# |w| tiles of a two-stage kernel spread anew over its stages, with three staging slots, and the last query blocks ordered by token block

## What is computed

```python
q = x @ Wq.T + bq;  k = x @ Wk.T + bk;  v = x @ Wv.T + bv      # 16 query heads, 4 kv heads, D = 128
sq, sk = elu(q) + 1, elu(k) + 1
kv = einsum('bhsd,bhse->bhde', sk, v);  k_sum = sk.sum(tokens)
attn = einsum('bhsd,bhde->bhse', sq, kv) / (sq . k_sum + 1e-6)
x = layernorm(x + attn @ Wo.T)

def absmean_quant(w):                    # ternary: -1, 0, 1
    scale = mean(abs(w))
    return sign(w) * (abs(w) >= 0.7 * scale)
h = gelu(x @ absmean_quant(w1).T + b1)                          # 2048 -> 8192
x = layernorm(x + h @ absmean_quant(w2).T + b2)                 # 8192 -> 2048
```

## Time and profile before

| | us |
|---|---|
| three runs | 2660.42, 2953.24, 2958.25 (median 2953.24) |
| profiled execution | 2657.98 |
| its span, slowest core (6) | 2656.4 |
| spans of the 8 cores | 2642.0 to 2656.4 |
| busy in the span: PE / DVE / ACT / POOL | 2506.3 / 892.9 / 608.0 / 274.2 |
| matmuls in the profile | 11628 |
| moved by DMA | 481.73 MB, mean 181 GB/s |

### The profile page before, as it was taken

The page is one execution under the profiler, slowest core; times in us unless marked ns, Lnnn a source line. Parts: engine busy times, 40 slices in busy tenths (PEclk is TensorE's granted clock), DMA queues, the critical chain, the costliest instruction groups (busy, mean ns, idle before and its releaser), DMA issues.

```text
span 2656.4 us, 30067 instructions; the slowest of 8 cores (2642.0 to 2656.4 us)
## 1 busy us (share of the span) xinstructions
PE 2506.3 (94%) x11628; PEld 1141.5 (43%) x11780; DVE 892.9 (34%) x906; ACT 608.0 (23%) x823; POOL 274.2 (10%) x333
## 2 busy tenths in 40 slices
PE   5999999978987988979999999999999999999998
PEld 1444444434443433334444444444444444444443
DVE  1222444425553444455577557311000000110022
ACT  0233677723333333321100000011121110000000
POOL 3000000013332000000122112100000000000000
PEclk9999999989999999989999999999999999999999
DMA  9984786677778887865688768527113110312252
GB/s 164 227 220 147 184 204 186 175 206 269 259 257 285 298 294 292 298 230 182 220 281 274 225 217 267 176 87 245 36 40 102 38 32 8 111 64 80 78 184 111
DMA packets 93339, 481.73 MB, mean 181 GB/s; under 512 B 11920, under 2 KB 11920, under 8 KB 50576
## 3 DMA queue, kind: packets, MB, share of 16 engines
q1 hardware_dynamic: 49824, 310.97, 35.3%
q0 software_dynamic: 33008, 145.77, 19.7%
q10 hardware_dynamic: 10368, 23.07, 3.3%
HBM read 431.53 MB, written 85.98 MB: 195 GB/s over the span
## 4 chain that ended last, share of the span: by engine, by line
PE 72%; DMA 19%; issue 4%; DVE 3%; ACT 1%; POOL 0%; ACTq 0%; SPq 0%; DVEq 0%; POOLq 0%
PE PB L617 27%; PE PB L595 22%; DMA MB<-w2h 14%; PE PB L515 8%; PE PB L631 4%; PE PB L488 4%; PE PB L478 4%; PE PB L552 2%; DMA R<-woh 2%; DMA MA<-w1h 1%; DMA RW<-wvh 1%; ACT MB L849 1%; DVE R L713 1%; DVE MB L710 1%; PE PB L503 0%
## 5 line engine op out<-in xcount | busy, mean ns | idle before, releaser
L617 PE MATMUL PB<-R 128*128 128x512 fp8e4 x2688 | 582.7, 379 | 0.3 <-DVE R L713 0.3
L595 PE MATMUL PB<-R,MC 128*128 128x512 bf16 x2006 | 450.3, 383 | 32.2 <-DVE MC L713 27.2
L617 PEld LDWEIGHTS PB<-R 128*128 128x128 bf16 x2688 | 262.8, 98 | 318.0 <-issue 1.2
L595 PEld LDWEIGHTS PB<-R,MC 128*128 128x128 fp8e4 x2048 | 200.0, 99 | 281.5 <-issue 50.4
L794 DVE TENSOR_TENSOR MC<-PB,MC 128x512 f32<-128x512 f32 x56 | 38.3, 684 | 822.2 <-PE PB L617 728.1
L595 PE MATMUL PB<-MA,MC 128*128 128x512 bf16 x1004 | 229.9, 379 | 1.1
L595 PE MATMUL PB<-MB,MC 128*128 128x512 bf16 x1003 | 229.9, 379 | 1.1
L515 PE MATMUL PB<-R,MB 128*128 128x512 bf16 x1003 | 229.5, 379 | 1.1
L710 DVE TENSOR_SCALAR MB<-MA,thr 128x2048 fp8e4<-128x2048 f32 x107 | 137.6, 1286 | 252.1 <-DMA MA<-w1h 146.3
L943 ACT ACTIVATE R<-PB,b_sb 128x512 bf16<-128x512 f32 x192 | 128.3, 684 | 402.5 <-PE PB L595 402.5
L849 ACT ACTIVATE MB<-MB 128x2048 f32<-128x2048 f32 x70 | 133.7, 1910 | 378.6 <-DMA MB<-w2h 336.9
(11 more groups left out here) (108 smaller groups left out, 1747.4 us busy)
## 6 DMA issues: line engine op xcount, KB each, us to landing
MA<-w1h SPq DMA_DIRECT2D x122, 1024.0 KB, 7.5
MB<-w2h SPq DMA_DIRECT2D x85, 1024.0 KB, 6.7
MA<-w2h SPq DMA_DIRECT2D x43, 1024.0 KB, 7.9
R<-xb POOLq DMA_DIRECT2D x32, 512.0 KB, 75.8
x1s<-R POOLq DMA_DIRECT2D x16, 1024.0 KB, 7.1
w1qd<-MC POOLq DMA_DIRECT2D x64, 256.0 KB, 5.2
MC<-w1qd SPq DMA_DIRECT2D x64, 256.0 KB, 2.6
R<-w2qd SPq DMA_DIRECT2D x16, 1024.0 KB, 5.8
```

What stands on the lines that cost most here:

```text
L595: ins = e.matmul(PB[F1_BANK[k % 4][t]], w1q_sb(k)[:, dc * 128:(dc + 1) * 128], x1T(s, t, dc), start=(dc == 0), stop=(dc == 15))
L617: ins = e.matmul(PB[F2_BANK[P][cc]], hid(fc)[:, c * 128:(c + 1) * 128], w2q_sb(s, g, q)[:, j * 512:(j + 1) * 512], start=(fc == 0), stop=( ...
```

## The change

1. |w| is dealt out anew: 32 tiles behind the k/v blocks (one each from block 6 on, two from block 26 on), 40 behind the projections (every second, and one more behind n = 6, 14, 22, ...), 24 behind Wo's items (every second up to 38, then 44, 50, 56, 62), and the last 32 tiles as 64 half tiles of 128 x 1024 in FFN1, three in two steps, until step 42. `wsum` has a column for each.
2. Slots: tiles 0 to 71 as before in MA's two; tiles 72 to 91 go through three, MA's two and MB's; 92 to 95 through MB's. The half tiles have three slots in MB, of which the third is the buffer of the cast `x1bf` and is loaded only after the last transposes.
3. The last three heads of the q stage (ic 13, 14, 15) are projected by token block: all three for t = 0, then t = 1, and so on. Their order is `QORD`.
4. Wo's second half goes to the blocks 0 and 1 of x and is asked for after projections 55 and 58; the residual slots move to blocks 2 and 3.
5. Wo's items begin with two chunks by column halves instead of three; threshold 1 is made at item 10; the first four w1 tiles are made ternary behind items 48, 52, 56 and 60.

```diff
-NW_KV = 26
-NW_Q = 32
-NW_WO = 32
-NW_F = 128 - NW_KV - NW_Q - NW_WO
+NW_KV = 32
+NW_Q = 40
+NW_WO = 24
...
+def w_behind_q(n):
+    a = NW_KV + n // 2 + (n + 1) // 8
+    return range(a, NW_KV + (n + 1) // 2 + (n + 2) // 8)
...
+def w_behind_f(k):
+
+    return range(min(NW_HALF, 3 * k // 2), min(NW_HALF, 3 * (k + 1) // 2))
...
+QORD = [(ic, t) for ic in range(13) for t in range(4)]
+QORD += [(ic, t) for t in range(4) for ic in range(13, 16)]
...
+ITEMS = [(0, 0), (0, 1), (1, 0), (1, 1), (0, 2), (0, 3), (1, 2), (1, 3)]
+ITEMS += [(c, g) for c in range(2, NCH) for g in range(4)]
...
-THR1_ITEM = 22
+THR1_ITEM = 10
 W1_PRE = 4
-PRE_ITEM = [36, 40, 44, 48]
+PRE_ITEM = [48, 52, 56, 60]
...
+    def stage_half(u):
+        o = (0, 1024, 3072)[u % 3]
+        return mbf[:, o:o + 1024]
...
+        def load_w(i):
+            if W_PREV[i] >= 0:
+                e.wait_ge(a_abs, W_PREV[i] + 1)
+            e.dma_start(out=stage(w_slot(i)), in_=w_tile(i)).then_inc(d_st[w_slot(i)], 16)
+
...
+        def load_half(u):
+            if u < 2:
+                e.wait_ge(a_abs, NW_FULL)
+            elif u == 2:
+                e.wait_ge(t_tr, 2 * NCH)
+            else:
+                e.wait_ge(a_abs, NW_FULL + u - 2)
+            e.dma_start(out=stage_half(u), in_=w_half(u)).then_inc(d_h[u % 3], 16)
+
         for k in range(W1_PRE, NFC):
             e.wait_ge(v_w1, k - 1)
             e.dma_start(out=stage(k % 2), in_=w1h[k]).then_inc(d_st[k % 2], 16)
-            i = NW_ATT + NW_WO + k - W1_PRE
-            if i < 128:
-                e.wait_ge(a_abs, i)
-                e.dma_start(out=stage(2), in_=w_tile(i)).then_inc(d_st[2], 16)
+            if k == W1_PRE:
+                load_half(0)
+                load_half(1)
+            if k == W1_PRE + 1:
+                load_half(2)
+            if k >= 6:
+                for u in w_behind_f(k - 6):
+                    if u + 3 < NW_HALF:
+                        load_half(u + 3)
...
-                e.wait_ge(t_q, 62 + pr // 4)
+                e.wait_ge(t_q, 55 + 3 * (pr // 4))
```

More of the change, by code:

```diff
@@ L171, in wo_sb @@
     def wo_sb(ic, g):
-        base, o = (rw, 0) if g < 2 else (r1, 8192)
+        base, o = (rw, 0) if g < 2 else (r1, 0)
         o += ic * 1024 + (g % 2) * 512
@@ L176, in wo_pair @@
     def wo_pair(half, pr):
-        base, o = (rw, 0) if half == 0 else (r1, 8192)
+        base, o = (rw, 0) if half == 0 else (r1, 0)
         return base[:, o + pr * 2048: o + (pr + 1) * 2048]
     def yslot(c):
-        o = (0, 2048, 12288)[c % 3]
+        o = 8192 + (c % 3) * 2048
         return r1f[:, o:o + 2048]
@@ L255, in build_nc, with w_half @@
     p_id, p_b2 = sem("p_id"), sem("p_b2")
-    def n_slot(i, j):
-        return i // 2 + 1 if i < NW_ATT else i - NW_ATT + 1
-    def abs_slot(i):
-        return i % 2 if i < NW_ATT else 2
-    N_ST = [NW_ATT // 2, NW_ATT // 2, 128 - NW_ATT]
+    N_THR = [0, 5, 11]
+    N_W = [16 * (1 + sum(w_slot(b) == w_slot(i) for b in range(i))) for i in range(NW_FULL)]
+    W_PREV = [max([b for b in range(i) if w_slot(b) == w_slot(i)], default=-1) for i in range(NW_FULL)]
+    N_ST = [sum(w_slot(b) == j for b in range(NW_FULL)) for j in range(3)]
     def w_tile(i):
         return w1h[i] if i < 64 else w2h[(i - 64) // 16, (i - 64) % 16]
+    def w_half(u):
+        return w_tile(NW_FULL + u // 2)[:, (u % 2) * 1024:(u % 2 + 1) * 1024]
     def w1_load_no(k):
@@ L507, in tensor_program @@
         e.wait_ge(v_kb, NSC)
-        for n in range(64):
-            ic, t = n // 4, n % 4
+        for n, (ic, t) in enumerate(QORD):
             if n >= 3:
@@ L672, in normalise @@
             e.wait_ge(a_r, m + 1)
-            e.tensor_tensor(attn(m % 4, m // 4), PB[3 + m % 2], rn(m), ALU.mult).then_inc(v_at)
+            e.tensor_tensor(attn(QORD[m][1], QORD[m][0]), PB[3 + m % 2], rn(m), ALU.mult).then_inc(v_at)
         e.wait_ge(v_sv, NSC)
-        for n in range(64):
-            ic = n // 4
+        for n, (ic, t) in enumerate(QORD):
             e.wait_ge(a_eq, n + 1)
@@ L856, in scalar_program @@
             e.activation(ek(sc), kb1(sc), AF.Exp, bias=c_none).then_inc(a_e)
[L857 to L858 removed]
+            for i in w_behind_kv(sc):
+                abs_tile(i)
         def inverse(m):
@@ L879, in scalar_program @@
                 inverse(n - 3)
-            if n % 2 == 1:
-                abs_tile(NW_KV + n // 2)
+            for i in w_behind_q(n):
+                abs_tile(i)
         inverse(61)
@@ L909, in scalar_program @@
                 evict_x1T(ENDS[i - 4])
-            if i % 2 == 0:
-                abs_tile(NW_ATT + i // 2)
+            for w in w_behind_wo(i):
+                abs_tile(w)
         chunk_rstd(15)
@@ L946, in scalar_program @@
                     evict_x1T(15)
-                if s == 0 and k < NW_F:
-                    abs_tile(NW_ATT + NW_WO + k)
+                if s == 0:
+                    for u in w_behind_f(k):
+                        abs_half(u)
                 if s == 1 and k == 3:
```

96 lines of the change are left out of this document (59 added, 37 removed).

## The result

The changed kernel takes **2576.5 us** where the kernel before, beside it on the same chip, takes 2660 to 2665. The ratio is 0.966, 95% interval 0.963 to 0.969: 3.4% faster. The forecast was 2566 us, its range 2548 to 2600.

What follows compares the result with a forecast made beforehand. TensorE's matmuls bound the kernel, with some 64 us lost in FFN1 and 55 in Wo to waits and slower clock. 2658.0 - 52.4 (FFN1) - 49 (Wo) + 7.4 (q) + 2 (k/v) = 2566 us, range 2548 to 2600.

Steps and rivals of the forecast that it cites:

- threshold 2: FFN1's first half, step 48: TensorE waits 4.7 us for the ternary and then the sum, plus 2 us of slow clock.
- group 55: q stage: while Wo's second half streams, a landing takes 10 us, the tile is 4.4 late, 3.5 us at TensorE.
- x1T's wait: FFN1, before step 3: half 2 is asked for only after the last transposes, so TensorE waits 3.5 us.
- 38 x 1.2 = 46 of the 64: FFN1 before the change: 38 steps of 8.1 us instead of 6.9 make 46 of some 64 us lost.
- GpSimd's loop: Wo: add, store, wait and reload of residual slots takes 16.2 us against chunks of 14.7; 5 us allowed.
- The wait of group 63: End of the q stage: a late tile while Wo's second half streams makes TensorE wait 3 us.
- A: FFN1 becomes bound by w1's two slots, from a landing of 9.7 us; at 11, 28 us more: 2594; chance 0.13.
- B: Wo: POOL's residual loop bounds all 13 reloads at 16.2 us a chunk, 19.5 instead of 5: 2581; chance 0.10.
- C: q stage: 40 tiles through two slots make the kernel slower than before; at a landing of 18 us, 2713; chance 0.02.
- D: FFN1: halves each take a whole tile's 5.9 us, one behind another, 86 us more: 2652; chance 0.03.
- E: q stage: Wo's second half or the late triples of tiles cost double, about 15 us more: 2581; chance 0.06.
- F: Wo and q stage come without the prediction's allowances: 2550 us; chance 0.04.

Runs made afterwards that it cites:

- The experiment with one slot: Changed kernel with FFN1's last 32 tiles whole through one slot, each load asked for when the sum before is out: 2606.6 us, ratio 0.9772 to the kernel before.
- the run with q's tail moved: Changed kernel with the three tiles behind groups 54, 62 and 63 of the q stage moved into Wo (37 and 27 tiles): ratio 0.9647 to the kernel before.
- k/v spread: Changed kernel with the six extra k/v tiles behind blocks 20, 22, ... 30 instead of 26 to 31: ratio 0.9675 to the kernel before.
- with 31 tiles: Changed kernel with 31 tiles in the q stage instead of 40 and 33 in Wo instead of 24: ratio 0.9693 to the kernel before.
- 31 tiles and threshold 2 first: Changed kernel with 31 q tiles, threshold 2 ahead of the ternary, x1T copied out behind step 1: 0.967; with k/v's extra tiles spread too: 0.9664.
- four edits: Changed kernel with threshold 2 ahead of the ternary, k/v tiles spread, three q tiles in Wo, last x1T copied out behind step 1: 2562.4 us, ratio 0.961.

## Why the forecast was nearly right, and what it missed

**The step that failed: the slow clock behind the short waits.** The prediction priced it at one place only, 2 us behind threshold 2, and at nothing behind every other wait that it foresaw, in k/v, in q, in Wo and before step 3. On core 1 it was 2.7 us behind the last k/v products, 1.4 at group 55, 5.4 in Wo and 3.8 in FFN1, 13.3 instead of 2. These 11 us are as much as the 10.6 of gain that did not come; the other errors nearly cancel. The waits and the mechanisms were mostly those named. The first of the four is hidden in the q stage. TensorE's timeline on core 1, where the products had waited 3.36 us, and on core 0, where they had waited 0.95 (one matmul's record is missing there):

```profile
275.16 13.21 PE L577 MATMUL PB<-R,MB 128*128 128x512 bf16 x48
```

```profile
270.14 10.52 PE L577 MATMUL PB<-R,MB 128*128 128x512 bf16 x47
```

The first attention pair comes 13.05 us after the stage's start on core 1 and 10.36 on core 0. The granted clock of core 1 was 0.82 from 275.16 to 290.60 us, and 1.00 on core 0.

**FFN1, -52.4 forecast, -50.7 measured.** The sum of what stays was right in each term that has a row: a step of 6.95 us, x1T's wait 3.58 against 3.5 (2.9 to 4.7 by core), threshold 2's 4.68 against 4.7 on all eight cores. The clock was put at 2 and is 3.8 (455.1 - 443.0 - 3.58 - 4.68): it was counted behind the threshold and not behind x1T's wait. What the prediction said of the loss before, "38 x 1.2 = 46 of the 64", is wrong in size. The rows said so already: TensorE's waits for ternaries were 27.2 in 24, not 46. The experiment with one slot gives 24 for 32 steps, since the lead of the ternary tiles pays for the first steps. The forecast escaped this because it was built from what remains and not from what goes.

**The halves.** The price per half was the open question, and the rule on transfers under 1 MiB that the prediction cites spoke against them. The run with one load in flight shows that a half lands in 4.9 us where a whole tile takes 5.9, so a large part of a landing does not depend on size. A line through these two landings, with other traffic beside them, puts that part at 4.9 - (5.9 - 4.9) = 3.9 us, an estimate. The Trainium skill, DMA: Bandwidth & Descriptors, section Anatomy of one DMA, has such a fixed part, about 2 us, for transfers issued by GpSimd; these are issued by SyncE, and come out larger. The decision, that depth hides it, was right. The transfers were asked for two steps ahead, landed in 10.4 us each, and TensorE did not wait. That whole tiles with as many bytes in flight would have done as well is not excluded by any run.

**Wo, -49 forecast, -39.2 measured on core 1.** This is the term that was furthest off. Weights hidden: right, they were there at 543, before the item at 551.6. Chunks of 14.7 to 15.5: right for eleven of fourteen, all at 14.7; the other three are 16.2 to 18.2 apart. GpSimd's loop was no bound; the allowance of 5 us for it was met by one late residual, for which VectorE waited 10.8 us:

```profile
599.36 1.86 PE L593 MATMUL PB<-ident,MB 128*128 128x128 bf16 x16 [3.36 <-DVE MB L829]
601.01 8.97 PE L614 MATMUL PB<-RW,R 128*128 128x512 bf16 x32
```

Two things were not in the sum. The wait of group 63 (3.0 in the prediction's q stage, 4.18 here) falls behind the first Wo items, so it is Wo's, and the clock behind the small waits was priced at nothing. The second line above shows it: 32 matmuls in 8.97 us instead of 7.07. The same core after the other two (timelines, first column the start, second the length):

```profile
513.19 5.06 PE L577 MATMUL PB<-R,MB 128*128 128x512 bf16 x16
```

```profile
541.86 0.58 PE L564 MATMUL PB<-MC,ksrep 128*128 128x512 bf16 x1 [4.18 <-DVE R L735]
...
542.66 9.13 PE L614 MATMUL PB<-RW,R 128*128 128x512 bf16 x32
```

16 in 5.06 instead of 3.62, and 32 in 9.13: 1.4 to 2.1 us behind these waits of 2.6 to 4.2, where some matmuls ran at the 1.2 GHz level. Not every such wait has that cost: in the run with the old q order the wait of 2.65 before the first Wo item is followed by 16 matmuls in 3.61, at full clock. In the run with one slot, waits of 0.5 to 1.5 us were each followed by 32 matmuls in 7.07, with no such cost. Wo's 250.7 is 235.8 of work (core 0 of the run with q's tail moved: 238.0 less 2.2 of waits, at a granted clock of 1.00), 9.5 of waits and 5.4 of clock. The forecast had 235, 6 of waits and no clock. On the other cores Wo took 244 to 250; core 1 had the longest.

**q, +7.4 forecast, +4.4 measured.** The sum is nearly right by luck. Core 1 did not wait at groups 8, 16, 24 or 32 at all (forecast 3.6), and waited 2.58 at group 55 (forecast 3.5) with 1.4 of clock; group 63's wait is Wo's, and the 2.7 of clock behind k/v, which was not forecast, took its place. The 2.65 before the first Wo item went as forecast. Together that is 2.58 + 1.4 + 2.7 - 2.65 = 4.0 of the 4.4. At group 55 ScalarE had waited for its tile, whose load took 13 us beside the stream of Wo's weights (ScalarE's timeline):

```profile
507.70 1.91 ACT L918 ACTIVATE MA<-MA 128x2048 f32<-128x2048 f32 x1 [3.40 <-DMA MA<-w2h]
```

The prediction had 10 for it. Cores 2, 3 and 5 did wait near group 12, up to 3.2, but there by the debt from k/v. The experiments with k/v spread and with 31 tiles point to one cause behind both: 40 tiles in two slots are just too many for the core of two neighbours that has the longer landings, so a wait taken away in one place turns up in the next. Of two neighbours one has tile landings 0.2 to 1 us longer in q by their medians; that was the late one in all four pairs of the changed kernel, and in three of four when it ran again. The prediction read one core's landings as those of all.

**k/v, +2 forecast, +4.4 measured on core 1.** The last products wait 3.36 us there, 1 to 4 by core, where all cores had waited 0.95 before. So the wait grew by 2.4, near the forecast, and it goes when the tiles are spread: the mechanism (9 us for two tiles against blocks of 7.1) was right. Of the other 2.0 some 0.7 are waits for the first loads, and 1.3 are not accounted for.

**The missing 10.6 us** are then: 2.4 in k/v, 9.8 in Wo and 1.7 in FFN1, less 3.0 in q and 0.3 in the rest. Counted by cause, slow clock is 11 of them. With q's tail moved, the waits at the end of q and in Wo and the clock behind them go, and some 7.5 us with them. What is not settled is which neighbour is the late one and why it alternates from run to run.

**Rivals.** A: not in the changed kernel (w1's median 8.5); seen on one core of the fastest one and on five of each kernel with 31 tiles and threshold 2 first. B: no, but true with 33 tiles in Wo. C: no; the q stage stayed at 258 or less. D: no, and true with one load in flight. E: in small part; the two waits of q's end cost 10.3 us with their clock on core 1 where 6.5 were priced, not 15 more. F: 2550 without allowances is nearly what four edits reach, 0.961 of 2658, or 2554.

## What to carry to other kernels

Build a forecast from the work and waits that will remain, not from the loss you think goes: a chain that turns too slowly costs TensorE only from where its lead is used up. Splitting a transfer gains only with more of them in flight; with one in flight, half a tile took 83% of a tile's time here. And read all cores before you price a stage that is near the limit of its slots: the slowest core was mostly one with the longer landings, a wait removed there came back a few groups later, and a wait of TensorE of 2.6 to 4.7 us can cost 1.4 to 2.7 us of slow clock besides. Price that clock with each wait: here it was the size of the forecast's whole error.
